# A fused transformer block: GpSimd normalises by mean times reciprocal deviation, and each engine's critical wait is written first

## The reference

```
x = x + attn_a(layernorm(x))
x = x + ffn(layernorm(x))
x = x + attn_b(layernorm(x))
x = x + ffn(layernorm(x))

layernorm(x) = (x - mean) / sqrt(var + 1e-5)
attn_a: q = x @ Wq + bq (16 heads of 8), k, v = x @ Wk + bk, x @ Wv + bv (2 heads);
        blocks of 32 rows look at a window of 64 keys, masked to u in [t, t + 32); softmax; @ Wo + bo
attn_b: q, k = elu(.) + 1;  out = (q @ (k^T v)) / (q @ sum(k) + 1e-6);  @ Wproj + bproj
ffn:    h = butterfly(x @ W_exp + b_exp, up); h = gelu(h + up_bias); h = butterfly(h, down);
        y = h @ W_con + b_con + down_bias
```

## Time and profile before

| | |
|---|---|
| median of 3 runs | 560.13 us (557.11 to 562.09) |
| span of the profiled execution | 560.6 us, 14708 instructions |
| PE busy | 525.0 us (94%) |
| DVE busy | 441.2 us (79%) |
| POOL busy | 450.9 us (80%) |
| ACT busy | 358.7 us (64%) |
| mean granted TensorE clock | 0.978 of full speed |

### The profile page before, as it was taken

How to read it: one execution, slowest core, us unless ns; L and a number is a source line. 1 busy time by engine, 2 the same in 40 slices (tenths; PEclk the granted TensorE clock), 3 DMA queues, 4 the chain that set the end, 5 groups by cost and what they waited for, 6 DMA issues and landing times. The chain is left out here.

```text
span 560.6 us, 14708 instructions
## 1 busy us (share of the span) xinstructions
PE 525.0 (94%) x5060; PEld 345.8 (62%) x5060; DVE 441.2 (79%) x1272; ACT 358.7 (64%) x578; POOL 450.9 (80%) x646
## 2 busy tenths in 40 slices
PE   5786998979999999999999999999999999999795
PEld 3442554546766666666667676666666667777563
DVE  5778789897888989898988898888989797663341
ACT  2543376567687767676777768686767777664532
POOL 6665689899898999999898989899999797955420
PEclk9789799989999999999999999999999999999899
DMA  9533232322223232232313231323232222100001
GB/s 310 170 76 81 63 83 54 81 74 56 54 58 80 62 76 66 68 78 48 102 45 87 63 87 44 84 60 77 61 76 50 59 66 58 39 1 20 1 20 37
DMA packets 49546, 38.88 MB, mean 69 GB/s; under 512 B 12352, under 2 KB 38976, under 8 KB 49472
## 3 DMA queue, kind: packets, MB, share of 16 engines
q1 hardware_dynamic: 47024, 33.73, 23.9%
q10 hardware_dynamic: 2448, 4.22, 2.1%
HBM read 15.64 MB, written 5.51 MB: 38 GB/s over the span
## 5 line engine op out<-in xcount | busy, mean ns | idle before, releaser
L501 POOL TENSOR_TENSOR probs_t<-probs_t,first 128x1024 f32<-128x1024 f32 x64 | 151.3, 2367 | 11.5 <-DMA probs_t<-probs_t 11.5
L645 PEld LDWEIGHTS ring<-w,early 128*128 128x128 f32 x1024 | 119.0, 192 | 9.6 <-issue 7.0
L982 ACT ACTIVATE early<-ring,b 128x512 f32<-128x512 f32 x128 | 87.2, 684 | 54.7 <-PE ring L633 53.1
L645 PE MATMUL ring<-w,early 128*128 128x128 f32 x1024 | 120.0, 275 | 0.8 <-ACT early L982 0.8
L972 ACT ACT_TABLE_LOAD x58 | 74.4, 1283 | 10.7 <-issue 9.7
L601 PE MATMUL ps_s<-kx,q_t 64*32 64x512 f32 x960 | 65.9, 606 | 3.4 <-DVE merged L1268 2.7
L633 PE MATMUL ring<-xT_G,w1b 128*128 128x512 f32 x128 | 67.1, 612 | 0.7 <-ACT xT_G L960 0.7
L991 ACT ACTIVATE probs_t<-merged_t 128x1024 f32<-128x1024 f32 x64 | 65.3, 1044 | 3.8 <-DVE merged_t L1275 3.7
L633 PE MATMUL ring<-xT_F,w1b 128*128 128x512 f32 x128 | 59.9, 611 | 0.4 <-ACT xT_F L960 0.4
L1255 DVE COPY_PREDICATED ps_s<-first,ps_s 128x512 f32<-128x512 uint32 x64 | 43.6, 681 | 9.2 <-PE ps_s L601 9.0
L1282 DVE STREAM_TRANSPOSE ps_o<-ps_o 128x512 f32<-128x512 f32 x64 | 46.2, 722 | 1.6 <-PE ps_o L618 0.3
(11 more groups left out here) (124 smaller groups left out, 1023.9 us busy)
## 6 DMA issues: line engine op xcount, KB each, us to landing
probs_t<-probs_t SPq DMA_DIRECT2D x256, 64.0 KB, 2.0
kx<-kv_rows SPq DMA_DIRECT2D x120, 40.0 KB, 2.2
x_P<-in_x SPq DMA_DIRECT2D x16, 256.0 KB, 3.2
out_x<-x_G SPq DMA_DIRECT2D x16, 256.0 KB, 2.4
vx_t<-kv_rows SPq DMA_DIRECT2D x128, 8.0 KB
up_s<-in_up_m ACTq DMA_DIRECT2D x7, 256.0 KB, 8.4
down_s<-in_down_m ACTq DMA_DIRECT2D x7, 256.0 KB, 8.4
kv_rows<-kv_t SPq DMA_DIRECT2D x16, 80.0 KB, 2.8
```

The lines of the kernel that those rows point to most:

```text
L501: nc.gpsimd.tensor_tensor(parts, parts, keep.rearrange("p (a t) -> p a t", a=1).to_broadcast([P, PAIR * HEADS, WIN]), ALU.mult).then_inc(p ...
L645: last = nc.tensor.matmul(bank(name)[:, P * j:P * (j + 1)], hid[s][:, c, P * j:P * (j + 1)], w2[:, c], start=(c == 0), stop=(c == CH - 1))
L982: nc.scalar.activation(hid[s][:, c], bank(name)[:], ACT.Gelu, bias=b1[:, c:c + 1]).then_inc(drained[BANK[name]].sem, 1)
```

## The change

Two edits. In `normalise` on POOL the negated mean nm is gone: the product is now mr = mean x rstd, and the last step is xn = x x rstd - mr, by multiply and subtract instead of multiply and add. rv and rstd are made by a function of their own, `rooted_variance`, which stands alone where DVE makes xn, so that the three unused products go too. The semaphore is called `rooted`.

And in nearly every step the critical wait, for what was made last, is now written first. Waits on the same semaphore are joined to one with the higher value (`Count.both`). The turns are renumbered per engine, and steps of a function are split into functions; the order of instructions on PE, DVE, ACT and SP is the same, row for row, and on POOL too but for the instructions taken out. A few pairs are added to COVERED, which lists waits that need not be written, and the waits for the first scores and weighted values change places as below.

```diff
             def normalise(g, s):
 
-                if g == 0:
-                    pool.wait_ge(half_set, 1)
-                pool.wait_ge(vec.sem, vec.after(g, f"{s}.mv"))
-                pool.wait_ge(pool_step.sem, pool_step.after(g - 1, f"{s}.nmr"))
-                nc.gpsimd.tensor_scalar(rv[s][:], mv[s][:, :, 1], LN_EPS, None, ALU.add
-                                        ).then_inc(pool_step.sem, 1)
-                nc.gpsimd.tensor_scalar(nm[s][:], mv[s][:, :, 0], -1.0, None, ALU.mult).then_inc(pool_step.sem, 1)
-                pool.wait_ge(pool_step.sem, pool_step.after(g, f"{s}.rv"))
-                nc.gpsimd.tensor_tensor(rstd[s][:], rv[s][:], half[:], ALU.pow).then_inc(pool_step.sem, 1)
-                pool.wait_ge(pool_step.sem, pool_step.after(g, f"{s}.nm", f"{s}.rstd"))
-                nc.gpsimd.tensor_tensor(nmr[s][:], nm[s][:], rstd[s][:], ALU.mult).then_inc(pool_step.sem, 1)
-                if (g == 0 and s == "P") or (g == NG - 1 and s in "FL"):
-                    return
+                rooted_variance(g, s)
+                pool.wait_ge(rooted.sem, rooted.after(g, f"{s}.rstd"))
+                nc.gpsimd.tensor_tensor(mr[s][:], mv[s][:, :, 0], rstd[s][:], ALU.mult).then_inc(rooted.sem, 1)
+                pool.wait_ge(rooted.sem, rooted.after(g, f"{s}.mr"))
                 pool.wait_ge(product.sem, product.after(g - 1, TURNED[s]))
-                pool.wait_ge(pool_step.sem, pool_step.after(g, f"{s}.nmr"))
                 for j in range(TILES):
                     last = nc.gpsimd.tensor_scalar(xn[s][:, j], x_of(g, s)[:, j], rstd[s][:, j:j + 1],
-                                                   nmr[s][:, j:j + 1], ALU.mult, ALU.add)
+                                                   mr[s][:, j:j + 1], ALU.mult, ALU.subtract)
                 last.then_inc(normed.sem, 1)
...
+            def rooted_variance(g, s):
+                pool.wait_ge(vec.sem, vec.after(g, f"{s}.mv"))
+                nc.gpsimd.tensor_scalar(rv[s][:], mv[s][:, :, 1], LN_EPS, None, ALU.add).then_inc(rooted.sem, 1)
+                pool.wait_ge(rooted.sem, rooted.after(g, f"{s}.rv"))
...
+                nc.gpsimd.tensor_tensor(rstd[s][:], rv[s][:], half[:], ALU.pow).then_inc(rooted.sem, 1)
...
             def copy_out(g, name, dst, *freed):
 
-                act.wait_ge(product.sem, product.after(g - 1, *freed))
-                act.wait_ge(product.sem, product.after(g, name))
+                act.wait_ge(product.sem, product.both((g, name), *((g - 1, user) for user in freed)))
...
             def row_max(g, j):
+                dve.wait_ge(vec.sem, vec.after(g, f"W.cp{j}"))
                 dve.wait_ge(drained["S"].sem, drained["S"].after(g - 1, f"W.S{j}"))
-                dve.wait_ge(vec.sem, vec.after(g, f"W.cp{j}"))
...
             def weighted_values(g, j):
 
                 name = f"W.PV{j}"
-                if j == 0:
+                pe.wait_ge(parted.sem, parted.after(g, f"W.um{j}"))
+                if (name, "values") not in COVERED:
                     pe.wait_ge(vec.sem, vec.after(g, "W.vx"))
-                pe.wait_ge(parted.sem, parted.after(g, f"W.um{j}"))
```

More of the change, by code:

```diff
@@ L145, in after, with both @@
         return max(self.value(group, name) for name in names)
+    def both(self, *events):
+        return max(self.value(group, name) for group, name in events)
     def value(self, group, name):
@@ new lines, in turn @@
+                for g in due(t, 5):
+                    add_bias(g, "F", bproj_s, "F.down", "L.proj")
+                for g in due(t, 2, 2):
+                    add_bias(g, "P", bo_s, None, "W.proj")
+                for g in due(t, 4, 2):
+                    normalise(g, "W")
+                for g in due(t, 3, 0, 1):
+                    probs_parted(g, 2)
+                for g in due(t, 4, 0, 1):
+                    add_bias(g, "W", bffn_s, "W.proj", "F.down")
+                for g in due(t, 6, 0, 14):
+                    normalise(g, "L")
@@ new lines, in turn @@
+                for g in due(t, 3, 2):
+                    probs_parted(g, 2)
+                for g in due(t, 6):
+                    add_bias(g, "L", bffn_s, "L.proj", "G.down")
+                if t == 20:
+                    rooted_variance(15, "L")
+                for g in due(t, 4, 2):
+                    add_bias(g, "W", bffn_s, "W.proj", "F.down")
+                if t == 19:
+                    rooted_variance(15, "F")
+                for g in due(t, 3, 1):
+                    probs_parted(g, 3)
@@ new lines, in turn @@
+                for g in due(t, 5):
+                    norm_transposed(g, "F", "W")
+                for g in due(t, 3, 2):
+                    scores(g, 2)
+                for g in due(t, 4, 2):
+                    weighted_values(g, 1)
+                for g in due(t, 6):
+                    linear_state(g)
+                for g in due(t, 5):
+                    ffn_up(g, "F", 3)
+                    ffn_up(g, "F", 2)
+                    ffn_up(g, "F", 0)
+                    ffn_up(g, "F", 1)
@@ new lines, in turn @@
+                for g in due(t, 6, 0, 14):
+                    linear_out(g, 0)
+                for g in due(t, 7):
+                    norm_transposed(g, "G", "L")
+                if t == 21:
+                    linear_out(15, 0)
+                for g in due(t, 3, 1):
+                    scores(g, 3)
+                for g in due(t, 4):
+                    weighted_values(g, 2)
+                for g in due(t, 2, 2):
+                    attention_q(g)
+                for g in due(t, 5):
+                    ffn_down(g, "F")
@@ L791, in turn @@
-                for g in due(t, 10):
-                    linear_kv_rows(g, 0)
-                if t == 8:
+                    up_stage(3, "a")
+                    up_stage(3, "b")
+                    up_stage(4, "a")
+                    scores(0, 2)
+                    up_stage(5, "a")
+                    down_stage(1)
+                    scores(0, 3)
+                    attention_q(1)
+                    weighted_values(0, 0)
+                    down_stage(2)
+                    up_stage(4, "b")
@@ new lines, in turn @@
+                    scores(1, 0)
+                    up_stage(6, "a")
+                if t == 0:
+                    up_stage(2, "a")
+                    first_keys(1)
+                    scores(0, 0)
+                    norm_transposed(1, "P", "P")
+                    down_stage(0)
+                for g in due(t, 4, 0, 1):
+                    weighted_values(g, 3)
+                for g in due(t, 6, 0, 14):
+                    linear_out(g, 1)
+                for g in due(t, 7, 0, 14):
+                    ffn_up(g, "G", 3)
@@ new lines, in turn @@
+                if t == 21:
+                    linear_out(15, 1)
+                for g in due(t, 1, 2):
+                    norm_transposed(g, "P", "P")
+                if t == 4:
+                    heads_transposed(0)
+                if t == 3:
+                    down_stage(3)
+                    scores(1, 1)
+                    down_stage(4)
+                for g in due(t, 4, 2):
+                    weighted_values(g, 3)
+                for g in due(t, 2, 2):
+                    scores(g, 0)
@@ L1209, in moments @@
                     dve.wait_ge(x_in[g % 2], 16 * (g // 2 + 1))
+                else:
+                    own = drained[BANK[MADE[s]]]
+                    dve.wait_ge(own.sem, own.after(g, MADE[s]))
                 dve.wait_ge(vec.sem, vec.after(g - 1, f"{s}.mv"))
```

761 lines of the change are left out of this document (305 added, 456 removed), and 77 rows, old and new, of tables (COVERED, PRODUCTS, VECTOR).

## The result

The changed kernel takes 597.07 us (median of four runs, 595.92 to 599.23) against 561.11 for the kernel before (four runs, 557.11 to 562.66): a ratio of 1.065, 95% interval [1.061, 1.070]. It is slower by 36 us. The prediction was 555.0 us, with 560.0 at the top of its range.

The account below looks back on a forecast made before the run. PE was taken to bound the middle, where the change gives 0, and chains of DVE, ACT and POOL the head and tail; 3.49 us from the head and 1.60 from the tail, 5.1 off 560.13, gave 555.0 us, range 551.5 to 560.

Parts of the forecast that it names:

- the price of the form that had no row: POOL's last normalisation step: four multiply-subtracts taken at the 1.74 us of four multiply-adds.
- the upper end of 2.84: POOL's last normalisation step, at worst multiply-add plus a separate addition: 3.3 us lost over 3 normalisations, leaving a 1.8 gain.
- these 15 us of POOL: Middle of the span: POOL's work on the removed small instructions is hidden by PE, so removing it gives 0 there.
- signs that the prediction named for being wrong: PE gaps in the middle, head shortened by less than 2 us, or new 0.50 clock stretches in the head.
- The end chain: Tail from 496 us: ACT copies or gelus, DVE additions and pairs, and two last normalisations save 1.60 us.
- DVE's wait for the reciprocal deviation: Before the last normalisation in the tail: 1.73 us should become about 1.45, saving 0.27.
- The pairs of the head: 28 DVE instructions in the head waiting for their own predecessor save 0.07 us each, 1.96 in all.
- POOL's wait before xn: Normalisation on POOL: carrying the wait on the instruction saves 0.10 us, part of 0.31 per normalisation on the chain.
- The 3.5 us expected in the head: Head: DVE pairs 1.96, DVE after PE 0.36, ACT waits 0.24 and three POOL normalisations 0.93, together 3.49 us saved.
- Rival 1: PE's low-clock stretches near 124 us and in the tail vanish: 551.6 us if both, 553.3 if one; chance 0.22.
- Rival 2: Head gains little because POOL or transfers between engines hold its chain: 558.5 us, at the outside 560.1; chance 0.23.
- Rival 3: PE's swapped waits hold up its run-ahead in the middle's 12 turns: 565.8 us at 0.9 a turn; chance 0.05.

Follow-up runs that it names:

- e2: The kernel before with only the last normalisation step made multiply and subtract (small product from mean times 1.0), same instructions and waits: 622.27 us, ratio 1.111.
- e1: The changed kernel with its new waits, but the negated mean and multiply-add of the kernel before in all four normalisations: 551.93 us, ratio 0.986.

## Why the prediction was wrong

**The step that failed** is the price of the form that had no row: "I take the 1.74 us of four multiply-adds, since operands and shapes are the same". It takes 3.14 (800 ns for each of the four instead of 451), in the changed kernel as in e2, where every other instruction and wait is that of the kernel before. Even the upper end of 2.84 was too low. A bound "from the nearest rows" was no bound here, because the duration belongs to the pair of operations and not to operands and shapes, and none of the rows had a slow pair.

**A second mistake stands behind it**; without it the case would have stayed in sight. The upper end was applied to 3 normalisations on the chain of the head only ("3.3 in all"), and for the middle the text said "In the middle these 15 us of POOL are hidden by PE". That holds for what is taken away. It does not hold for what may be added: 2.84 instead of 1.74 for 4 normalisations is 4.4 us a turn, less 1.2 for nm and the wait before xn, on the 29.49 us that POOL's own turn takes: 32.7 us, more than PE's 30.24, and over 12 turns, less the 5.1 gained, a kernel slower by some 25 us. The rival on the other side was looked for in TensorE's waits and got 0.05; POOL as the new bound was not on the list, though the earlier trace rows show it idle for only 2.3 of 30 us, and a third of that was waiting for others. Two of the signs that the prediction named for being wrong came: PE has gaps in the middle, and the head is shorter by less than 2 us.

**The end chain: right.** The steps that the prediction named for the tail came out at their size. Three pieces of the changed kernel's chain in the tail (start, us, what):

```profile
578.37 0.08 issue
578.45 0.24 POOL rv_L L445
578.70 0.07 issue
578.77 1.05 POOL rstd_L L449
579.82 0.03 issue
...
581.68 0.02 issue
...
590.68 0.02 issue
```

DVE's wait for the reciprocal deviation, 1.73 us in the earlier trace rows, is 0.08 + 0.24 + 0.07 + 1.05 + 0.03 = 1.47, for 1.45 predicted. The copy of xT_G on ACT starts 0.02 after PE (581.68) where it was 0.08, a saving of 0.06 as predicted; the last residual 0.02 (590.68) where it was 0.12, so 0.10 for the 0.09 that was only bounded. DVEq and ACTq are gone from there. From the end of PE's long wait for o_l to the end of the span it was 560.6 - 522.5 = 38.1 us and is 594.1 - 557.1 = 37.0: 1.1 shorter, for 1.6 predicted from 496 us on.

**The pairs of the head: right in size.** The first scores of the changed kernel on DVE (timeline), beside the earlier trace rows:

```profile
20.14 0.70 DVE L1187 COPY_PREDICATED ps_s<-first,ps_s 128x512 f32<-128x512 uint32 x1 [0.55 <-PE ps_s L605]
20.87 0.69 DVE L1194 TENSOR_REDUCE rowmax<-ps_s 128x16 f32<-128x512 f32 x1
```

20.14 + 0.70 to 20.87 is 0.03, where it was 0.10: the 0.07 of the prediction. POOL's wait before xn gave a little less than the 0.10 assumed: mr_P starts at 235.46 and takes 0.20, xn_P starts at 235.77, which is 0.11 later where it was 0.19.

**Head, middle and tail of the whole change.** Cut at PE's third transposition of xn_W (121.96 before, 121.58 changed, 113.95 in e1) and at the end of its wait for o_l (522.5, 557.1, 512.4), the head is 0.4 us shorter, the middle 435.5 instead of 400.5 us, the tail 1.1 shorter: -0.4 + 35.0 - 1.1 = 33.5, the difference of the spans. The 3.5 us expected in the head are not there in the changed kernel: e1, without the slow form, reaches the same point 7.6 us earlier. So the head had gained what was forecast and more, and the slow form took it back. (These are single executions; up to 130 us the kernel before had 20.5 us at the lower clock, the changed one 6.8 and e1 none, so not all of the gain is that of the waits.) In the middle, 12 turns of 33.51 - 30.24 are 39 us, less what the first and last turns differ.

**The rivals.** Rival 1 (the lower clock goes too) comes nearest for the half of the change that gains, with 551.6 to 553.3 forecast and, with nm kept, 551.9 and 552.2 measured. But the size is partly luck: it went off the two stretches of the earlier trace rows, and the larger ones lie before 62 us. The one in the tail is still there in e1's profile (512 to 516 us). Rival 2 (only the tail moves) had a head that gains little, and so it came out, 0.4 us, but by the slow form and not for its reason: in e1, with the new waits and POOL's old form, the head is shorter by 8.0 us. Rival 3 (PE loses in the middle) found no support, since the turn is 30.23 with the new waits of PE.

## What to carry to other kernels

An operation that has no row in the trace is not priced by a neighbour with the same shapes: time it alone first, in a kernel of a few lines, since a single changed operation code can double it. For an engine that now lies under the bound, write down its open time per turn, and hold against it the upper end of every price that the change puts on that engine in the middle too; busy 80% of the span meant 0.75 us of room in a turn of 30. And where a change has two halves, give each its own sum: here one gained 8 us and the other lost 45.

## What the runs showed of the hardware

On GpSimd the scalar instruction with two operations was fast for three of the twelve pairs timed, multiply-add, add-multiply and multiply-multiply (447 to 455 ns for 128x128 with scalars from memory; multiply-add takes 0.83 ns for each further element of a row); the nine others take 789 to 801 ns, and multiply-subtract 3.33 ns for each further element. A lone operation is slower than such a pair, 602 against 448 ns with a scalar from memory, 533 against 301 with a fixed number. On VectorE the three pairs timed (multiply-add, multiply-subtract, subtract-multiply) take 341 to 342 ns. With VectorE running the same kind of instruction beside it, multiply-add on GpSimd took 610 ns instead of 448, multiply-subtract 915 instead of 792, and VectorE's own instruction 363 instead of 342. In the block, where VectorE is busy 26.3 of 30 us with other instructions, it is hardly seen: the multiply-adds there have a mean of 451 ns. The Trainium skill, GPSIMD Engine Reference, section Performance pitfalls for Q7 kernels, gives 4 cycles an element for a dependent chain of fp32 operations; with the 1.2 GHz of its section Elementwise — side-by-side cycle accounting that is an estimate of 3.33 ns, the slope measured here for the slow pair. That the slow pairs run as such a chain is only argued, no run shows it.

A wait that an instruction carries itself wakes DVE 0.02 to 0.04 us after its releaser, one that the sequencer takes 0.10 to 0.12; on ACT it is 0.02 and 0.08, on POOL before xn 0.11 and 0.19.

Stretches at the lower level of TensorE's clock come and go between executions of the same program, and the time goes with them: 562.8 us at a mean clock of 0.979, 557.3 at 0.990 and 0.991, which is 1% and more than the 4.4 us that the waits gain at equal clock. Comparing executions at equal mean clock keeps the two apart.
